# Routed expert loop of a fused attention and mixture kernel: down products ahead of the inner rows' transposition, address words held in registers, one unread product fewer per late head

## The reference, cut to what matters

```python
x = x + _L0_xattn_ref(_layernorm(x), ctx, ctx, ...)   # 8 heads, decay matrix D = exp(log_D - max)
x = x + _L0_ffn_ref(_layernorm(x), ...)               # 32 routed experts, top 4, and a shared one
x = x + _L1_xattn_ref(ctx, _layernorm(x), ...)        # a long convolution by FFT, and two small FFNs
x = x + _L1_ffn_ref(_layernorm(x), ...)               # 8 dense experts of width 1024
```

```python
qk = jnp.einsum('bhsd,bhtd->bhst', qh, kh) / jnp.sqrt(jnp.float32(dh))
C = qk * D
h = jnp.einsum('bhst,bhtd->bhsd', C / (normalizer + EPS_BACKEND), vh)
```

```python
scores = jax.nn.softmax(xf @ Wg, axis=-1)
weights, indices = jax.lax.top_k(scores, TOP_K)        # 4 of 32 experts for each of 2048 rows
out = swiglu(xf[tok], W1[e], W3[e], W2[e]) * w[:, None]   # silu(x @ w1) * (x @ w3) @ w2
y = y.at[tok].add(out)
```

## Time and profile before

| | |
|---|---|
| median of three runs | 1689.5 us |
| the profiled execution, and its span | 1688.0 us, 1686.2 us |
| TensorE busy | 1560.1 us (93%) |
| VectorE, ScalarE, GpSimd busy | 71%, 52%, 39% |
| mean granted TensorE clock | 0.969 of full speed |

### The profile page before, as it was taken

The page is one execution under the profiler, slowest core; times in us unless marked ns, Lnnn a source line. Parts: engine busy times, 40 slices in busy tenths (PEclk is TensorE's granted clock), DMA queues, the critical chain, the costliest instruction groups (busy, mean ns, idle before and its releaser), DMA issues.

```text
span 1686.2 us, 26019 instructions
## 1 busy us (share of the span) xinstructions
PE 1560.1 (93%) x7986; PEld 1282.0 (76%) x7986; DVE 1190.6 (71%) x2226; ACT 877.2 (52%) x1548; POOL 660.8 (39%) x585
## 2 busy tenths in 40 slices
PE   6999997769993889899999999999999999999998
PEld 5797673358882678778888888888888888888887
DVE  6656877836665689777667777767777776776776
ACT  4455332124432346655665665665656755756653
POOL 2453156688805652440540530621612603604400
PEclk9998998989996899999999999999999999999999
DMA  6996012168843212000100100101101101001001
GB/s 197 274 310 236 10 70 99 57 200 256 266 141 120 85 51 75 1 1 27 57 32 32 64 6 32 69 0 50 50 0 50 50 13 56 32 13 57 32 13 51
DMA packets 74493, 136.38 MB, mean 81 GB/s; under 512 B 8592, under 2 KB 52176, under 8 KB 74256
## 3 DMA queue, kind: packets, MB, share of 16 engines
q1 hardware_dynamic: 40544, 92.76, 17.0%
q10 hardware_dynamic: 27696, 25.51, 4.7%
q0 software_dynamic: 6144, 16.79, 3.1%
HBM read 90.93 MB, written 44.11 MB: 80 GB/s over the span
## 4 chain that ended last, share of the span: by engine, by line
PE 55%; DVE 1%; ACT 1%; issue 0%; DVEq 0%; ACTq 0%
PE ps L2569 35%; PE ps L2589 18%; PE ps L2585 1%; DVE eF L1344 0%; DVE gU L1356 0%; PE ps L2601 0%; DVE x L1458 0%; PE ps L2495 0%; ACT eH L1831 0%; PE ps L2496 0%; DVE tL L1149 0%; ACT gU L1815 0%; DVE tF L1140 0%; ACT tH L1693 0%; ACT L1729 0%
## 5 line engine op out<-in xcount | busy, mean ns | idle before, releaser
L1356 DVE TENSOR_TENSOR gU<-ps,gU 128x512 f32<-128x512 f32 x384 | 257.2, 687 | 96.4 <-PE ps L2569 69.3
L2044 POOL TENSOR_TENSOR cL<-cR,cH 128x384 fp32r<-128x384 f32 x192 | 208.0, 1107 | 214.6 <-ACT cH L1735 214.6
L1349 DVE TENSOR_TENSOR eL<-eF,eH 128x512 fp32r<-128x512 f32 x256 | 186.1, 727 | 141.5 <-ACT eH L1831 141.3
L1815 ACT ACTIVATE gU<-ps 128x512 f32<-128x512 f32 x384 | 227.1, 597 | 105.9 <-PE ps L2569 91.7
L1831 ACT ACTIVATE eH<-eF 128x512 fp32r<-128x512 f32 x256 | 161.2, 630 | 159.8 <-DVE eF L1344 159.5
L2569 PE MATMUL ps<-xTH,cH 128*128 128x512 f32 x512 | 201.0, 393 | 4.9 <-DVE gU L1356 3.9
L2569 PE MATMUL ps<-xTH,cL 128*128 128x512 f32 x512 | 199.8, 390 | 0.0
L2569 PE MATMUL ps<-xTL,cH 128*128 128x512 f32 x512 | 199.8, 390 | 0.0
L2031 POOL TENSOR_TENSOR cR<-cR 128x256 f32<-128x256 f32 x32 | 34.0, 1062 | 392.4 <-DMA cR<-in_w 392.4
L2589 PE MATMUL ps<-eH,cH 128*128 128x512 f32 x480 | 186.8, 389 | 0.0
L2589 PE MATMUL ps<-eH,cL 128*128 128x512 f32 x480 | 186.7, 389 | 0.0
(11 more groups left out here) (440 smaller groups left out, 3434.5 us busy)
## 6 DMA issues: line engine op xcount, KB each, us to landing
cR<-in_w SPq DMA_DIRECT2D x32, 768.0 KB, 4.2
slots_in<-eS SPq DMA_DIRECT2D x16, 768.0 KB, 11.0
eS<-in_wr SPq DMA_DIRECT2D x32, 384.0 KB, 4.0
xl<-slots_in ACTq DMA_DIRECT2D x48, 256.0 KB, 3.9
slots_out<-yo ACTq DMA_DIRECT2D x48, 256.0 KB, 3.1
cwB<-expert_weights SPq DMA_DIRECT2D x16, 512.0 KB, 3.6
k_parts<-parts SPq DMA_DIRECT2D x8, 512.0 KB, 5.6
q_parts<-parts SPq DMA_DIRECT2D x8, 512.0 KB, 4.0
```

Of the source, the lines that this page charges most:

```text
L1349: dve.tensor_tensor(eL[:, b, :], eF[:, b, :], f32(eH[:, b, :]), ALU.subtract).then_inc(block_low, 1)
L1356: dve.tensor_tensor(to[:, :], ps[:, 2 + half, :], to[:, :], ALU.add).then_inc(half_summed, 1)
L1815: act.activation(to[:, :], ps[:, half, :], ACT.Identity).then_inc(snap_done, 1)
L2044: last = pool.tensor_tensor(cL[c][:, cols_], cR[c][:, cols_], f32(cH[c][:, cols_]), ALU.subtract)
```

## The change

One unread product instead of two in the heads from the 21st on; all 13 loads of words in front of the loop, at six places among the transforms; and in each step of the loop the down products of pair q - 1 ahead of the inner rows' transposes of pair q. No product that is read is added or taken away.

```diff
-                spare(2 + i % 2, 4 if i < FILLED else 2)
+                spare(2 + i % 2, 4 if i < FILLED else 1)
...
+            held = []
+
+            def hold_words(count):
+                for it in range(len(held), len(held) + count):
+                    held.append(nc.values_load_multi_w_load_instructions(words[0:1, 4 * it:4 * it + 4], engines=[mybir.EngineType.PE],
+                                                                         min_val=0, max_val=(1 << 28) - 1)[1])
+
             pe.wait_ge(mul_done, 8)
             spectrum(0)
+            pe.wait_ge(table_step, 4)
+            hold_words(1)
             spectrum(1)
+            hold_words(2)
             pe.wait_ge(inverse_loaded, 16)
...
                     spare(0, 32)
                 inverse(n)
+                if n >= 3:
+                    hold_words((4, 2, PAIRS // 4 - 8)[n - 3])
...
-            ahead = load_words(0)
-            tile_up(0, 0, ahead[3])
-            wrap = ahead[0]
-            ahead = load_words(1)
+            tile_up(0, 0, held[0][3])
             for it in range(PAIRS // 4):
-                v = ahead
+                v = held[it + 1]
                 for j in range(4):
                     q = 4 * it + j
...
-                    if j == 2 and it + 2 <= PAIRS // 4:
-                        ahead = load_words(it + 2)
-                    hidden_transpose(q, j % 2)
                     if q:
                         tile_down(q - 1, (j + 1) % 2, v[j])
-            tile_down(PAIRS - 1, 1, wrap)
+                    hidden_transpose(q, j % 2)
+            tile_down(PAIRS - 1, 1, held[0][0])
```

More of the change, by code:

```diff
@@ L2354, in tile_transpose @@
                 return last.then_inc(tT_done, 1)
-            def load_words(it):
-                return nc.values_load_multi_w_load_instructions(words[0:1, 4 * it:4 * it + 4], engines=[mybir.EngineType.PE],
-                                                                min_val=0, max_val=(1 << 28) - 1)[1]
             def place(v):
```

## The result

| | before | changed kernel |
|---|---|---|
| median (6 runs each, on one chip) | 1689.62 us | 1669.95 us |
| lowest to highest | 1687.72 to 1696.95 | 1667.78 to 1672.40 |
| ratio, 95% interval | | 0.9879 [0.9859, 0.9899] |
| profiled execution, its span | 1688.0, 1686.2 us | 1672.4, 1670.6 us |
| TensorE busy | 1560.1 us (93%) | 1554.1 us (93%) |

The change takes 1.2% off the time, 19.7 us by the medians (the interval allows 17 to 24), where 22.4 was forecast. The profiled execution of the changed kernel is the slowest of its six.

The account below looks back on a forecast made before the run. TensorE, 93% busy, was taken as the bound; -17.2 + 0.5 - 1.4 + 1.5 - 1.7 + 0.3 - 4.4 = -22.4 us takes the profiled 1688.0 to 1665.6, median 1667 us, range 1661 to 1676.

Parts of the forecast that it names:

- The loads in the loop: Routed loop: removing all 11 loads of address words, which stop TensorE's sequencer, saves 17.2 us.
- late weights: Routed loop: weights that arrive late under the higher DMA traffic cost 0.5 us, bounds 0 and 5.
- Rival 1: The loop becomes bound by transfers and GpSimd, 7 to 8 us lost, 1674.5 us; chance 0.12.
- The start: Start of the routed loop: first up product sooner without a load before it, 1.7 us saved, bounds 0 and 2.4.
- The 13 loads in front: Among the transforms before the loop: the moved loads lie almost wholly in existing waits and cost 0.3 us.
- The order inside the loop: Each pair: TensorE returns from transposes to products once instead of twice, 0.03 us a pair, 1.4 us saved.
- The end of the loop: Last two pairs: one more latency of 1.47 us is exposed, costing 1.5 us, bounds 0.5 and 2.5.
- The heads: Late heads: one unread product less shortens the chain up to the loop by 4.4 us, bounds 0 and 7.3.
- the zeros: Behind the heads: stores of zeros, bound by the DMA engines, still land at 150.0; VectorE waits some 7 us.
- second wait: Behind the heads: VectorE's 4.49 us wait for ScalarE's squares goes, its reduction moving from 159.35 to 154.9.
- Rival 2: The heads' gain stops short: another chain ends last or the zeros move, 4.4 us gone, 1671.5 us; chance 0.12.
- rival 3: Late heads: the clock falls to 1.2 GHz with fewer unread products, all 44 costing 50 us, 1721 us; chance 0.06.

Follow-up runs that it names:

- e3_words_only: Kernel before with only the address words loaded in front of the loop; old order, two unread products; 1671.70 us, ratio 0.9883 to the kernel before.
- e4_heads_only: Kernel before with only one unread product instead of two in the late heads; 1684.74 us, ratio 0.9963 to the kernel before.
- e7_words_late: Changed kernel with all 13 loads of address words behind the last inverse; 1678.94 us, ratio 0.9929 to the kernel before.
- e2_old_order: Changed kernel with the inner rows' transposes ahead of the down products again; 1665.35 us, ratio 0.9837 to the kernel before.
- e9_scalar_unrolled: Changed kernel with ScalarE's loop over the pairs written out; 1670.24 us, ratio 0.9877 to the kernel before.
- e6_tail_old_order: Changed kernel with the old order in the last two steps of the loop only; 1668.10 us, ratio 0.9869 to the kernel before.
- e1_again: The changed kernel itself, unchanged, timed and profiled again; 1671.93 us, ratio 0.9869 to the kernel before.
- e10: Changed kernel with VectorE's wait for the zeros moved to in front of the rows' high and low parts; 1670.48 us, ratio 0.9884 to the kernel before.
- e11: As e10, and ScalarE squares the last batch ahead of its copy of the context product; 1669.36 us, ratio 0.9882 to the kernel before.
- e12: Changed kernel with the old order, the moved zeros wait and the squares ahead of the context copy; 1665.47 us, ratio 0.9856 to the kernel before.
- e8: Changed kernel with no unread product instead of one in the late heads; 1702.18 us, ratio 1.0071 to the kernel before.

## Why the prediction was right, and where not

**The loads in the loop, forecast -17.2.** e3_words_only gives 17.0. Right, and so was what stands behind it: GpSimd back to back, waits for TensorE 13.7 to 0.8 us, weights in time at a DMA share of 0.95. The 0.5 us for late weights were not needed. Rival 1 didn't come.

**The start, forecast -1.7:** 6.16 us at the first up product less 3.90 at the first transposes, 2.3. Its upper bound, 2.4, was nearer.

**The 13 loads in front, forecast +0.3:** nothing to be seen. In the changed kernel's trace the last of them ends at 340.6, and TensorE's next instruction waits for its rows until 345.85. The prediction had them run until 348.5, only 1.3 us ahead of the rows: it let the last four start when the last inverse has ended, but the sequencer reached them at 334.4, while the inverse ran. The first rows' load is 3.87 us sooner with the 13 and 3.75 without (e4_heads_only), which by the spread of the loop's start proves little alone. e7_words_late shows that it is their place that makes them free.

**The order inside the loop, forecast -1.4 with bounds 0 and 0.08 a pair.** This is the step that failed. The undisturbed pair takes 2.80 us in both orders, so the saved return from transposes to products is worth nothing; and it costs 2.0 us, 1.65 of them in every fourth pair. The prediction held the operands to be in time because the low parts end 1.47 us behind the inner rows' transposes and the down products start 2.0 behind them. That was true, and 0.5 us to spare looked enough. One pair of the changed kernel that no branch disturbs, all engines:

```profile
382.13 0.38 PE L2390 MATMUL ps<-ident,rh 128*128 128x128 f32 x2
...
383.04 0.42 DVE L1010 TENSOR_TENSOR rhL<-ps,rhH 128x256 fp32r<-128x256 f32 x1 [0.30 <-ACT rhH L1635]
383.28 0.60 ACT L1625 ACTIVATE hH<-ps 128x512 fp32r<-128x512 f32 x1 [0.27 <-PE ps L2365]
383.98 0.68 DVE L999 TENSOR_TENSOR hL<-ps,hH 128x512 fp32r<-128x512 f32 x1
384.21 0.28 PE L2400 MATMUL ps<-eHL,rhH 128*128 x1
385.58 0.36 PE L2381 MATMUL ps<-eHL,hH 128*128 x1
```

and of e2_old_order, from one pair's inner rows to the next one's up products:

```profile
385.94 0.38 PE L2390 MATMUL ps<-ident,rh 128*128 128x128 f32 x2
...
386.90 0.42 DVE L1010 TENSOR_TENSOR rhL<-ps,rhH 128x256 fp32r<-128x256 f32 x1
...
387.52 0.60 ACT L1625 ACTIVATE hH<-ps 128x512 fp32r<-128x512 f32 x1 [0.69 <-PE ps L2365]
...
388.15 0.69 DVE L999 TENSOR_TENSOR hL<-ps,hH 128x512 fp32r<-128x512 f32 x1 [0.23 <-ACT hH L1625]
...
388.88 0.36 PE L2400 MATMUL ps<-eHL,rhH 128*128 x1
...
390.04 0.36 PE L2381 MATMUL ps<-eHL,hH 128*128 x1
```

In the old order rhL ends at 387.32 and is needed at 388.88 (1.56 us to spare), hL ends at 388.84 and is needed at 390.04 (1.20). In the new order both transpositions end together, and ScalarE and VectorE get all their work of a pair at once: rhL has 0.75 us to spare (383.46 to 384.21) and hL 0.92 (384.66 to 385.58). ScalarE's stops at its loop's branches use that up: behind them hL has 0.32 to 0.41 us to spare in eight of nine pairs, and TensorE, which starts no sooner than 0.32 behind it, waits; in e2_old_order it has 0.77 or more at the branches, in e9_scalar_unrolled 0.91 or more. In the first stretched pair of the changed kernel (transposes at 376.19 and 379.42, 3.23 us) the stop was 1.01 us:

```profile
375.02 0.60 ACT L1625 ACTIVATE hH<-ps 128x512 fp32r<-128x512 f32 x1 [1.01 <-issue]
...
376.77 0.38 PE L2381 MATMUL ps<-eHL,hH 128*128 x1
...
378.30 0.38 PE L2400 MATMUL ps<-eHL,rhH 128*128 x1
```

hL (375.76 + 0.69) ends at 376.45. The up products start 0.58 us behind the pair's transposes instead of 0.36, and the down products take 0.90 us to the inner rows' transposes (379.20) instead of 0.72 in a pair of 2.80. In the seven other stretched pairs the up products start 0.35 to 0.37 behind as always, and the time goes into the down products, 0.84 to 0.95 us. e9_scalar_unrolled, which takes away only ScalarE's loop, shows the cause. Why the down products are slower behind a wait I read from the same place, and no run takes it apart: their eight register operations stand directly behind the up products, with no transposes between in which TensorE's sequencer could gain a lead.

**The end of the loop, forecast +1.5:** 2.2 us (10.50 for 8.31), inside its bounds. The prediction counted one more exposed latency of 1.47 us; there are two waits of 1.21 each where there was 0.17. e6_tail_old_order takes exactly this back.

**The heads, forecast -4.4:** 3.9 us at the first rows' load in the changed kernel, 3.75 with a whole of 4.9 in e4_heads_only, whose times say 6.2 [2.2, 10.3]. The size is inside the bounds, and that it lies so near the forecast is in part luck: the same instructions start the loop 7 us apart. The mechanism held for the most part. VectorE does stand 7.17 us for the zeros (3.6 to 7.5 in the six profiles that keep this wait), its second wait is gone (in e1_again 0.98 us of it are left), and its small operations set the reduction, 153.84 where 154.9 was forecast. That is 5.5 us sooner than before, 1.1 more than forecast; of these 1.6 us are lost again on the way to the first rows' load, where the clock differs between executions. Two reasons were wrong. The zeros do not land at 150.0 whatever TensorE does: with one unread product they land at 145.2 to 149.6 us (nine profiles), with two at 148.8 to 150.0 (three). And the zeros are not the last wall: take them away (e10) and the squares behind ScalarE's copy decide, take that away too (e11) and TensorE's own stretch at the low clock stands there. Rival 2 came in no more than that.

**The clock (rival 3, 0.06).** The changed kernel holds 1.00. But the prediction's reason against it, no idle time in the row, is wrong. All ten profiles with one unread product show a wait of 0.34 to 0.35 us for VectorE at 85 to 87 us, without harm, and TensorE can be faster than the stacks' loads, for which the prediction had 4.8 us under 5.2. Of the ten profiles with one product four show TensorE waiting for such a load at 99 to 101 us: 0.23, 0.69 and 1.03 us without harm (e12, e4, e7), and 1.18 us followed by 1.2 GHz for all the remaining heads (e9). With none a wait of 0.66 us for VectorE came ahead of it (e8). So the length of one wait alone doesn't tell whether the clock falls, and what does stays open. One of the 54 executions with one unread product lost its 40 us so; the rival had 1721 us, the execution took 1712.

**Sum.** -17.0 + 0 + 2.0 + 2.2 - 2.3 + 0 - 3.9 = -19.0, beside 19.7 by the medians and 19.8 at the end of the loop in the profile; the missing 0.8 lies mostly between the first up product and the fifth pair (7.81 us for 8.41). The 3.4 us by which -19.0 falls short of the forecast are what the order does inside the loop, +2.0 instead of -1.4. The other terms are off by 0.2 to 0.7 us each, and these errors cancel, which is luck.

## What to carry to other kernels

An operand that is ready in time is not enough: compare how long it is ready before it is needed in both orders, and hold that against the irregular stops of the engines that make it (a loop's branch, a DMA issue, the arithmetic for an address). An order that gathers an engine's transposes also gathers its consumers' work, and is paid again where the loop runs out. Work of a sequencer is free in front of a wait and costs its full time where the engine never waits: the loads of words on TensorE and the branches on ScalarE are two cases of it.

## What the runs showed of the hardware that was not expected

- A loop written as a loop costs ScalarE idle time before the high copy: 0.76 to 1.01 us behind eight of nine branches and 0.27 to 0.37 in its other pairs, where the unrolled code has 0.09 to 0.14 at a DMA share of 0.95 (e9_scalar_unrolled). In the old order the same branches cost the loop nothing that the profile shows.
- A load of four words and their checks holds TensorE's sequencer 1.45 to 1.74 us wherever it stands (1.56 a pair in the loop, 1.59 in e7_words_late). How far ahead the sequencer is depends on what is queued: 0.3 to 0.4 us in front of products of 0.12 us (ten of the thirteen loads of the kernel before), but 4.8 us in front of the last inverse's products of 0.59 us (331.9 to 336.7 in e7_words_late).
- Without unread products the heads fell to 1.2 GHz and stayed there for 90 us though TensorE was busy all the time (profiled once; the times of all eight executions are as late); with one, 53 executions of 54 show no such loss.
- Loads and order don't add up in the profiles: the order alone makes the loop 8.1 us longer in the kernel with loads in its loop (6.0 and 2.1, of which one pair at the low clock is 1.4), and 4.2 to 4.7 in the kernel without. The times (9.3 us by the medians, and 5 to 7) are too wide to tell this.
